# Turning the input by block loads and a VectorE transpose instead of TensorE, with the first layer norm folded into the weights

## What is computed

```
x = x + attention(layernorm(x))     # Q, K, V = x wq', x wk', x wv' (64 wide)
                                    # energy = K' V over the 1024 tokens of a batch
                                    # attention = (Q energy) sqrt(3/64) wo'
y = relu(layernorm(x) W_fc')**2 W_proj'        # 256 -> 1024 -> 256
x = x + count(5 steps: mem = 0.9 mem + y - reset; spike = mem > 1) / 5
layernorm(x) = (x - mean) / sqrt(var + 1e-5)   # no weights of its own
```

## Time and profile before

| | |
|---|---|
| median of 3 runs | 506.89 us (506.52 to 507.18) |
| the profiled execution | 509.51 us, of which its span is 507.7 us |
| PE busy | 487.9 us, 96% |
| DVE busy | 351.6 us, 69% |
| ACT, POOL busy | 284.9 us (56%), 208.0 us (41%) |
| DMA | 19.63 MB, 5792 packets, 10.4% of 16 engines' span |

### The profile page before, as it was taken

How to read it: one execution, slowest core, us unless ns; L and a number is a source line. 1 busy time by engine, 2 the same in 40 slices (tenths; PEclk the granted TensorE clock), 3 DMA queues, 4 the chain that set the end, 5 groups by cost and what they waited for, 6 DMA issues and landing times.

```text
span 507.7 us, 9333 instructions
## 1 busy us (share of the span) xinstructions
PE 487.9 (96%) x3124; PEld 441.4 (87%) x3124; DVE 351.6 (69%) x991; ACT 284.9 (56%) x519; POOL 208.0 (41%) x171
## 2 busy tenths in 40 slices
PE   6979799999999999999999999999999999999995
PEld 6768689898999998999999988999998999999995
DVE  5476457777777857777887776778777774939447
ACT  2526665656565565656556565655656575646540
POOL 2353344354344434434443533444343543445340
PEclk9889899999999999999999999999999999999998
DMA  8111001010111111011111101111100101010102
GB/s 290 71 43 41 1 1 43 21 63 2 43 41 43 44 43 41 1 41 41 42 41 41 42 0 44 41 41 41 42 0 0 41 1 43 0 43 2 42 1 83
DMA packets 5792, 19.63 MB, mean 39 GB/s; under 512 B 640, under 2 KB 1280, under 8 KB 5504
## 3 DMA queue, kind: packets, MB, share of 16 engines
q1 hardware_dynamic: 5760, 19.27, 10.4%
HBM read 10.88 MB, written 8.39 MB: 38 GB/s over the span
## 4 chain that ended last, share of the span: by engine, by line
PE 86%; DVE 7%; issue 4%; ACT 2%; DMA 1%; POOL 0%; DVEq 0%; ACTq 0%; POOLq 0%
PE hid_ps L739 11%; PE hid_ps L740 11%; PE hid_ps L741 11%; PE y_ps L741 11%; PE y_ps L739 11%; PE y_ps L740 11%; PE work_ps L779 3%; PE work_ps L764 2%; DVE stat L523 2%; PE kv_ps L739 2%; PE kv_ps L740 1%; PE kv_ps L741 1%; PE work_ps L845 1%; PE work_ps L846 1%; PE work_ps L739 1%
## 5 line engine op out<-in xcount | busy, mean ns | idle before, releaser
L312 POOL TENSOR_TENSOR hid_l<-hid,hid_h 128x512 fp32r<-128x512 f32 x128 | 165.6, 1298 | 258.4 <-ACT hid_h L363 258.4
L352 ACT ACTIVATE relu<-hid_ps 128x512 f32<-128x512 f32 x128 | 76.6, 599 | 123.9 <-PE hid_ps L741 123.9
L741 PE MATMUL y_ps<-wdn_h,hid_l 128*128 128x256 f32 x480 | 135.7, 283 | 0.0
L740 PE MATMUL y_ps<-wdn_l,hid_h 128*128 128x256 f32 x480 | 135.6, 283 | 0.0
L739 PE MATMUL y_ps<-wdn_h,hid_h 128*128 128x256 f32 x480 | 135.2, 282 | 0.0
L739 PE MATMUL hid_ps<-x2T_h,wup_h 128*128 128x512 f32 x256 | 107.1, 418 | 0.6 <-DVE x2T_l L576 0.3
L740 PE MATMUL hid_ps<-x2T_l,wup_h 128*128 128x512 f32 x256 | 100.8, 394 | 0.0
L741 PE MATMUL hid_ps<-x2T_h,wup_l 128*128 128x512 f32 x256 | 100.6, 393 | 0.0
L740 PEld LDWEIGHTS y_ps<-wdn_l,hid_h 128*128 128x128 f32 x480 | 91.3, 190 | 4.9
L739 PEld LDWEIGHTS y_ps<-wdn_h,hid_h 128*128 128x128 f32 x480 | 91.3, 190 | 4.9
L741 PEld LDWEIGHTS y_ps<-wdn_h,hid_l 128*128 128x128 f32 x480 | 91.3, 190 | 0.0
(11 more groups left out here) (116 smaller groups left out, 636.5 us busy)
## 6 DMA issues: line engine op xcount, KB each, us to landing
xs<-x_dram SPq DMA_DIRECT2D x15, 512.0 KB, 3.3
out_dram<-x SPq DMA_DIRECT2D x15, 512.0 KB, 2.7
hid<-w_up_dram SPq DMA_DIRECT2D x1, 1024.0 KB, 7.3
x<-w_down_dram SPq DMA_DIRECT2D x1, 1024.0 KB, 9.3
xs<-x_dram SPq DMA_DIRECT2D x2, 256.0 KB, 4.1
out_dram<-x SPq DMA_DIRECT2D x1, 256.0 KB, 2.0
out_dram<-x SPq DMA_DIRECT2D x2, 128.0 KB, 1.9
wkv_raw<-w_kv_dram SPq DMA_DIRECT2D x1, 128.0 KB, 5.4
```

The costliest lines, as they stand in the source:

```text
L312: nc.gpsimd.tensor_tensor(hid_l[:, i % 2, c, :], hid[:, c % 4, :], hid_h[:, i % 2, c, :].bitcast(f32), ALU.subtract).then_inc(hid_ready, 1)
L352: nc.scalar.activation(relu[:, c % 2, :], hid_ps[c % 2][:, :], ACT.Relu).then_inc(relu_done, 1)
L740: mm(dst, a[0], b[1], start=False, stop=False)
L741: return mm(dst, a[1], b[0], start=False, stop=stop)
```

## The change

Five things change together.

1. PE no longer turns the first norm in steps 0 to 12. For groups 3 to 15, SP loads the group a second time with eight DMAs of 32 partitions x 16 runs of 32 floats (128 bytes), laid so that one 32x32 VectorE transpose over 128x1024 gives raw x turned, in x2n. Groups 0 to 2 are turned by PE from xs.
2. What is turned is raw x. The mean is taken out of the weights instead: PE averages each weight column with a matrix of 1/256, and DVE subtracts that from wkv_raw and wqq_raw in place.
3. The deviation is applied later: k and v are scaled after they are turned back (`kv_scale`, one 128x512 instruction that reads kv_ps and a broadcast rstd1, into kv_scaled), and q's deviation by the residual, now four 128x256 instructions.
4. The normalise of the first norm is gone, with xn. ACT's high half and DVE's low half of the turned x now read x2n in SBUF, and stand earlier in the step (ACT at c = 1, DVE ahead of the residual).
5. The prologue is rewritten: wkv is loaded first, the moments of groups 2 and 3 move into step 0, and keep_warm's rounds go from 9, 2, 2, 2, 8, 2 to 4, 8, 4, 2, 16, 4.

```diff
+    x_blocks = x.rearrange("(g b q t) (k i e) -> g i k q t b e", b=4, q=32, t=TILES, k=EC, i=4)
...
+        def x_turned(r, n, k):
+            if by_matmul(r, n):
+                return turn_banks(n)[k][:, :]
+            return x2n[:, k * GROUP:(k + 1) * GROUP]
...
+            def load_blocks(r, n):
+                if not isinstance(r, int) or n > BY_MATMUL:
+                    sp.wait_ge(x_turn, upto(r, n - BY_MATMUL))
+                for i in range(4):
+                    for k in range(EC):
+                        dst = x_block[32 * i:32 * (i + 1), k * GROUP:(k + 1) * GROUP]
+                        sp.dma_start(dst.rearrange("q (t b e) -> q t b e", t=TILES, b=4), x_blocks[r * UNROLL + n, i, k])\
+                            .then_inc(x_block_loaded, 16)
...
             def step(r, i):
+                if there(r, i + RING) and not (isinstance(r, int) and i < 0):
+                    load_blocks(r, i + RING)
                 if there(r, i + RING + 1):
                     load(r, i + RING + 1)
...
             def kv_high_half(r, n):
-                act.wait_ge(kv_turned, upto(r, n + 1))
+                act.wait_ge(kv_in_scale, upto(r, n + 1))
...
-                    if c == 4 and there(r, i + 3):
-                        xnT_high_half(r, i + 3)
+                    if c == 1 and there(r, i + 3):
+                        xT_high_half(r, i + 3)
...
+            def kv_scale(r, n):
+                dve.wait_ge(kv_turned, upto(r, n + 1))
+                dve.wait_ge(rstd_ready[0], upto(r, n + 1))
+                if there(r, n - 1):
+                    dve.wait_ge(kv_ready, upto(r, n))
+                by_token = rstd1[:, n % RING, :].unsqueeze(2).broadcast_to([P, TILES, 2 * HEAD])
+                nc.vector.tensor_tensor(kv_scaled[:, :].rearrange("p (t d) -> p t d", t=TILES),
+                                        kv_bank(r, n)[:, :].rearrange("p (t d) -> p t d", t=TILES),
+                                        by_token, ALU.mult).then_inc(kv_in_scale, 1)
             def kv_low_half(r, n):
                 dve.wait_ge(kv_high, upto(r, n + 1))
-                src = kv_bank(r, n)[:, :].rearrange("p (a d) -> p a d", d=HEAD)
+                src = kv_scaled[:, :].rearrange("p (a d) -> p a d", d=HEAD)
...
             def residual(r, n):
-                for k in range(2):
-                    last = nc.vector.tensor_tensor(x1[:, n % RING, cols], work_ps[k][:, :], xs[:, n % RING, cols],
-                                                   ALU.add)
+                for t in range(TILES):
+                    last = nc.vector.scalar_tensor_tensor(x1[:, n % RING, cols], att, rstd1[:, n % RING, t:t + 1],
+                                                          xs[:, n % RING, cols], ALU.mult, ALU.add)
...
+            def turn_blocks(r, n):
+                dve.wait_ge(x_block_loaded, counted(r, BLOCK_LOADS * (n - BY_MATMUL + 1), BLOCK_LOADS * UNROLL))
+                dve.wait_ge(x2n_turned, upto(r, n - 2))
+                nc.vector.transpose(x2n[:, :], x_block[:, :]).then_inc(x_turn, 1)
...
-                    if c == 4 and there(r, i + 3):
-                        turn_first(r, i + 3)
...
-            keep_warm(8)
+            keep_warm(16)
             turn_second(0, 0)
-            keep_warm(2, work_ps[1])
+            keep_warm(4, work_ps[1])
```

More of the change, by code:

```diff
@@ L683, in step @@
                     energy_sum(r, i + 2)
-                if there(r, i + 3):
-                    normalise(r, i + 3, 0)
                 if there(r, i + 2) and closes_batch(i + 2):
                     eo_low_half(r, i + 2)
+                if there(r, i + 3):
+                    xT_low_half(r, i + 3)
                 if there(r, i + 1):
@@ L705, in step @@
                 if there(r, i + 3):
+                    kv_scale(r, i + 3)
                     kv_low_half(r, i + 3)
@@ L750, in turn_first, with average_weights, turn_second @@
             def turn_first(r, n):
-                if isinstance(r, int) and n == 2:
+                if n == 2:
                     pe.wait_ge(x2T_ready, 1)
-                if n >= 3 or not isinstance(r, int):
-                    pe.wait_ge(x1_ready, upto(r, n - 1))
+                for t in range(TILES):
+                    if n:
+                        pe.wait_ge(x_loaded[n], 16)
+                    elif t % 2 == 0:
+                        pe.wait_ge((first_pair_loaded, x_loaded[0])[t // 2], 16)
+                    for k in range(EC):
+                        at = t * EMB + k * P
+                        last = nc.tensor.transpose(turn_banks(n)[k][:, t * P:(t + 1) * P], xs[:, n, at:at + P], ident[:, :])
+                last.then_inc(first_x_turn, 1)
+            def average_weights(loaded, raw, first):
+                pe.wait_ge(loaded, 16)
+                for k in range(EC):
+                    last = mm((y_ps[0], e_ps)[first][:, 0:2 * HEAD], averager[:, :], raw[:, k * 2 * HEAD:(k + 1) * 2 * HEAD],
+                              start=(k == 0), stop=(k == EC - 1))
+                last.then_inc(mean_done, 1)
+            def turn_second(r, n):
                 for t in range(TILES):
                     if t % 2 == 0:
-                        pe.wait_ge(norm_ready[0], upto(r, n, 2, t // 2 + 1))
-                    for k in range(EC):
-                        at = t * EMB + k * P
-                        last = nc.tensor.transpose(turn_banks(r, n)[k][:, t * P:(t + 1) * P],
-                                                   (xn, x2n)[lane(r, n, 0)][:, at:at + P], ident[:, :])
-                last.then_inc(norm_turned[0], 1)
-            def turn_second(r, n):
-                if there(r, n + 2) and turn2_banks(r, n) is work_ps:
-                    pe.wait_ge(xnT_ready, upto(r, n + 3))
-                for t in range(TILES):
-                    if t % 2 == 0:
-                        pe.wait_ge(norm_ready[1], upto(r, n, 2, t // 2 + 1))
+                        pe.wait_ge(x2n_ready, upto(r, n, 2, t // 2 + 1))
                     for k in range(EC):
```

183 lines of the change are left out of this document (105 added, 78 removed).

## The result

The changed kernel takes 503.9 us in the median of 20 runs (500.79 to 507.44), the kernel before 506.89 (504.70 to 508.95, 20 runs). The ratio is 0.994, 95% interval 0.9922 to 0.9959: 0.6% faster, where 1.9% was forecast. The sign was right and the time lies just inside the range, but less than a third of the gain came.

The account below looks back on a forecast made before the run. PE's work bounds the kernel, other engines counting only where PE waits; 10.4 + 5.1 - 4.1 - 2.0 = 9.4 us less takes the median from 506.89 to 497.5 us, eight-in-ten range 491 to 504.

Parts of the forecast that it names:

- turnings, steps 1 to 12: PE no longer does a group's eight turnings, 0.87 us in each of steps 1 to 12: 10.4 us less.
- step 0: PE loses norm wait, turning and slow matmuls, 5.4 us less; DVE 1.0 us behind PE at group 2's energy sum.
- steps 5 and 9, longer wait: At a round's head the energy leaves DVE 2.05 us later, PE waits about 3.1 us: 4.1 us more in both.
- steps 3, 7, 11, beside the turnings: Energy 2.05 us later, less 0.53 given back and 0.86 of room: 0.66 us new wait each, 2.0 us more.
- The forecast's 0.7 for the prologue: First up chunk starts at 38.8 instead of 38.56 and takes 1.4 us instead of 2.34: gain 0.7 us.
- the hand-over: Handing over k and v in DVE's step, scaling included: low half of kv starts 0.91 us later than before.
- "more room": Step 1 has more room than steps 3, 7 and 11 for the later energy; no new wait was counted.
- "Prologue and step 0 together: 5.1 us.": Gain at the kernel's start: 5.4 from step 0, 0.7 from the prologue, less 1.0 for DVE behind PE.
- The rival of the clock: PE's clock falls after the 3.1 us waits in steps 5 and 9, about 1.3 us each: 500.1; chance 0.13.
- the rule: VectorE and GpSimd share an SBUF port pair; kv's low half waits for POOL: 0.91 us later, 0.40 without it.
- the line through the forecast's two rows: Block loads: line through 4 KB (162 ns) and 1 KB (48 ns) packets gives 14 ns per 128-byte run; taken as hidden.

Follow-up runs that it names:

- two variants: Changed kernel with VectorE's transpose behind the energy sum, 498.61 us; changed kernel with k and v not scaled from group 4 on, 499.96 us.
- the kernel with all pauses over 1.1 us removed from its body: Changed kernel with transpose behind energy sum, no loops, prologue's wait filled, fewer turnings, group 1's x first, against the kernel before: 488.80 us, ratio 0.9650.

## Why the forecast was wrong

Step by step, in us, from the start of each step's first up chunk in PE's timelines. For the prologue and step 0 the old kernel's column is the median of three profiles (the third is that of the old kernel without loops, whose prologue is the same), the new one's that of the seven with an unchanged prologue.

| term | forecast | before | after | measured |
|---|---|---|---|---|
| turnings, steps 1 to 12 | -10.4 | 28.89 (even steps) | 28.01 | -10.6 |
| prologue (start of the first up chunk) | +0.2 | 35.55, 37.38, 38.56 | 37.00 to 39.95, median 39.46 | +2.1 |
| step 0 | -5.4 + 1.0 - 0.9 | 24.13, 24.14, 26.11 | 21.47 | -2.7 |
| steps 5 and 9, longer wait | +4.1 | 1.07, 1.05 (wait) | 3.14, 3.12 (wait) | +4.1 |
| steps 3, 7, 11, beside the turnings | +2.0 | 29.31 | 29.11 | +2.0 |
| step 1, beside the turnings | 0 | 29.31 | 28.98 | +0.5 |
| fall of the clock behind steps 5 and 9 | 0 | none | one of two in each of six profiles | +1.5 |
| sum | -9.4 | | | -3.1 |

The forecast's 0.7 for the prologue was a start 0.2 us later (38.8 against 38.56) and a first up chunk 0.9 us shorter (1.4 against 2.34); that chunk lies in step 0, so the table has the 0.9 there.

The medians differ by 3.0. That the sum comes so close is partly luck: it rests on few profiles, and the median clock of the changed kernel's 20 runs, 0.9875, is below that of all its profiles.

From step 2 on the forecast's terms came out, two of them with luck. In steps 5 and 9 the wait grew by 2.07 us where 2.05 was forecast, but the hand-over was 0.77 later instead of 0.91, and VectorE stood for 2.65 us between the rounds instead of 2.49. In steps 3, 7 and 11 the forecast took the price for a wait of 0.66 us; PE's row shows a wait of 0.40, and where the transpose stands behind the energy and the wait is gone, the step is 0.67 shorter. So these steps lose more than their wait. In step 1 the forecast had "more room" and put nothing; there PE waits 0.27 us for the energy and the step gains 0.33 instead of 0.88.

Two steps of the forecast failed.

**"Prologue and step 0 together: 5.1 us."** The forecast for the new kernel was fair: first up chunk at 38.8, and its profiles have 37.00 to 39.95; step 0 at 26.11 - 5.3 = 20.8, and they have 21.47. The base was not. The profiled execution of before had the lower clock at 12 to 17, 32 to 41 and 54 to 58 us, and the second profile only at 32 to 36. So 2.0 us of step 0 (26.11 against 24.13 and 24.14) were an event of that one execution, and so were up to 3.0 of the 38.56 us of the prologue. The forecast said that the profiled time "stood 2.6 above the median" and carried this excess over unchanged. But the excess sat in the very stretch that the change rewrites: it was counted as gain first and as excess again. Of the 6.3 us that are missing, 4.5 lie in these two rows of the table: 1.2 + 2.0 = 3.2 in the base (38.56 and 26.11 against the medians 37.38 and 24.14), and 0.7 + 0.7 = 1.4 in the new kernel.

In the new prologue two things were missed beside that. The raw x of group 1 is needed before any norm, and in five of nine profiles it comes 1.0 to 1.6 us late. And a wait of 1.77 us for the low half of k and v, ahead of which the scaling now stands, has a fall behind it in eight of nine profiles.

**The rival of the clock, chance 0.13, "about 1.3 each".** Mechanism and price were right: a step with a fall takes 33.26 to 33.34 instead of 31.65 to 31.90 us, about 1.5 more. The chance was not: the forecast left the rival out of its sum, and it happened in each of the six profiles that have these waits unfilled, once, in step 5 or in step 9.

The Trainium skill (SBUF — State Buffer, SBUF: two separate sides) was weighed for the low half of k and v. The row has 1.02 us instead of 0.69; it starts at 174.26 and a `hid_l` of POOL lasts until 174.73, and the same instruction takes 0.69 at 63.99, where POOL is idle. That agrees with the shared port. The whole hand-over, scaling included, came 0.77 us later, between the 0.40 without the rule and the 0.91 with it.

The block loads' 128-byte runs cost about what the line through the forecast's two rows gave, 14 ns (14.7 by its figures of 48 and 162). Between 154 and 160 us, 230 GB/s x 2 us = 460 KB moved, 3594 runs, in (0.42 + 0.50 + 0.56) x 2 x 16 = 47.4 us of engine time: 13.2 ns each. DMA: Bandwidth & Descriptors, Specifications, of the Trainium skill wants 512 bytes or more for line rate; 128 bytes in 13.2 ns against 4 KB in the 162 ns of the prediction agrees, at 0.38 of the rate. It cost nothing that a profile shows: two sets for each group changed no step, and a group has about 24 us for them.

Not settled: why the fall came behind only one of the two equal waits of 3.1 us, and where the runs at 0.980 lose their clock, since no profiled execution of the changed kernel or of its variants was below 0.989.

## What to carry to other kernels

Before a stall of one profiled execution is counted as gain, look whether the execution stands above the median, and where the excess lies; two or three profiles of the same kernel cost little and show which pauses are followed by the lower clock. A longer pause of PE elsewhere can cost twice, once by its length and often once by the clock behind it. Turnings of the identity in such a pause are worth trying, and no pause is better: the kernel with all pauses over 1.1 us removed from its body ran 3.5% faster than before and within 1.0 us from run to run.

## What the runs showed of the hardware

- In the changed kernel and its variants, pauses of PE of 1.77 to 2.46 us were followed by the lower clock in 12 of 13 cases (prologue 8 of 9, steps 5 and 9 of two variants 4 of 4), and those of 2.96 to 3.20 us in steps 5 and 9 in 6 of 12. The waits of 0.99 to 1.62 us for x in the prologue and those of 1.03 to 1.07 us in step 0 were followed by none.
- In the three profiles of the old kernel, with or without loops, the prologue's pause of 3.13 to 3.20 us ahead of the turning of the second norm was followed by the lower clock in all three, one of 1.93 us ahead of it in two, and the one of 3.23 us in step 0 in one; those of 1.05 to 1.20 us in steps 5 and 9 in none of four. So the length of a pause alone doesn't tell whether the clock falls.
- While PE did nothing but turn the identity, the granted clock stayed at 1.00: 64 turnings for 7.15 us in the prologue, and 24 for 2.78 us in steps 5 and 9, with no fall behind them.
- VectorE's 32x32 transpose of 128x1024 float32 took 1229 to 1245 ns in all 13 groups.
- A run of 128 bytes cost 13 ns of a DMA engine, by the estimate above, and twice as many changed no step by more than 0.03 us.
